# A graph network on one core: unscaled second 16-bit parts in the build, and a new order at the layer changes and at the end of attention

## The chip, the cores and the metric

One Trainium2 chip, one of its cores (core 0). The metric is the device time of one execution of the program in microseconds (us).

## What is computed

Four residual blocks on x (2048 nodes x 512) over 67584 edges that are sorted by target (65536 random ones and 2048 loops). Each starts with h = max(layernorm(x), 0):

```python
x = x + attention(h)            # 32 graphs of 64 nodes, 8 heads; biases edge_attr @ We + be
                                # are added to the scores at (graph, source, target) of each edge
x = x + gcn3(h)                 # three times A1 @ (h @ W) + b, relu between; A1 from degrees
x = x + relu(A2 @ (h @ W.T + b))
x = x + relu(A3 @ (h @ weight)) # A3: edge_weight summed by (row, column)
```

## The kernel before

The nodes are 16 tiles of 128 (NT). 32-bit values that go through cheap products are held as two 16-bit parts: a first part (value x scale, rounded) and a second part (what the rounding left).

**The build** (`build_*`, once in these runs) turns the edge list into dense matrices with products of one-hot matrices, while PE also computes attention's projections. 1024 units of two nodes lie in 8 groups of 128; a unit's edges lie on the 128 partitions, and 16 units are a batch: 64 batches, n = 0 to 63. Per batch and engine:
- DVE, `hots(n)`: five products or comparisons that make the one-hot matrices, for sources (L706), for counts and weights (L701, L714) and for biases (L704, L719). They are held twice (n % 2). Then `evacuate(n - 1)`: the bias sums (L731) and the weight sums (L747) leave PSUM, as second part / 2^11 + what ACT has copied.
- PE: `project` pieces (L979 for q and k up to batch 41, L972 for v after it; zero to two pieces a batch by a fixed table; each piece is four 32-bit products, issued as eight instructions), now and then the turning of h (`turn_h`, L954), then 16 products of 256 columns for the biases (L996), 16 of 96 columns for counts and weights (L1001), and the turning of sums (`turn_weights`, L945). At batches with n % 8 = 3 the next group's fields are turned too (L933), and with n % 8 = 0 there is one product for the in-degrees (L994). Before L996, PE waits until `hots(n)` is made and the bias sums of n - 1 have left PSUM; before L1001, until the weight sums of n - 1 have.
- ACT: it copies projected pieces, the first parts of the sums (`copy_sums`: L843 biases, L849 counts, L850 weights), turned sums (L837) and the normed h (`relu`, L854). At n % 8 = 3 it makes the first parts of the next group (`copy_part`, part 0, L825 and L826); at n % 8 = 5 DVE makes the rest in 32 bits in place (`residual`, L685 and L686), and ACT scales it by 2^11 (`copy_part`, part 1, again L825 and L826). DVE's next group waits for that.
- SP stores pieces and sums, and loads x and h.

The second part is scaled by 2^11 (LOW), so its sums can't be added to the first part's in PSUM: columns of both stand side by side in `hot_eb` and in the bank.

**Attention** (`attention_*`) runs in periods t over tiles: PE turns probabilities of t + 1 (L1311), projects tile t (`output`, L1341), mixes t + 1 (L1329) and scores t + 4 (L1300). In the last two periods ACT also prepares the first graph layer: in t = 14 four `weight_hi` (L1657) and two `relu` (L1673), ahead of the copy of the mixed tile 15 (`copy_mixed`, L1247) for which `output(15)` waits; in t = 15 `copy_turned` and `split_hi` for tiles 0 and 1, then two more `relu`. PE turns tiles 0 and 1 (L1866) ahead of `output(15)`, and 2 and 3 behind it.

**Layers** 0 to 4 each have `products` (h @ W; 12 products a tile, L1923: first x first, first x second, second x first) and `sums` (aggregation, L1989, 16 tiles x 2 parts x 16 blocks). In layers 1 and 2, h is split by a power of two that comes from its largest value: DVE's `h_scale` (L2171 and on), one `peak_row` (L1872) and one `peak_all` (L1879) on PE. The last of the four column chunks is scaled while products 0 to 2 run: after product 0 stands `peak_row`, after product 1 `peak_all`. PE asks for tile t + 1 two products before the end of tile t (`await_parts`): its second part, and the result of tile t - 2 having left its bank. ACT and DVE split tile 3 in their turn t = 3, after the results of tile 0. In layer 3 two products with one row of ones (L1919) put the bias into PSUM, one for each 16-bit part. `between` places single PE instructions among the sums by their number.

Of the kernel before, what the change touches and what calls it, by code (L numbers as in the profile page):

```python
# [18 lines left out]
H = 8  # L19
# [480 lines left out]
LOW = float(2 ** 11)  # L500
# [24 lines left out]
def build_memory(nc, keep, m):  # L525
# [11 lines left out]
    m.bias_first = place("bias_first", [P, NT, H], F32, AT_REST + 23040)  # L537
# [8 lines left out]
    m.bias_new = m.stage[:, 0:2].rearrange("p z (two t h) -> p z two t h", two=2, h=H)[:, :, 0]  # L546
# [5 lines left out]
BUILD_SEMS = "got read turned copied rest keyed parts hots batch bias_done first_part first_bias slab biased chunk new dve store0 store1"  # L552
# [103 lines left out]
def build_dve(nc, io, keep, m, s, first_round):  # L656
# [64 lines left out]
    def evacuate(n):  # L721

        nonlocal k
        q = n // 4
        sums = m.bias_ps[:, 0:NT * HP].rearrange("p (t two h) -> p two t h", t=NT, two=2)
        out = keep.bias[:].rearrange("p (h t) m -> p t h m", h=H)[:, :, :, n]
        dve.wait_ge(s["first_bias"], n + 1)
        if n % NBATCH == 0:
            dve.tensor_tensor(keep.deg[:], m.deg_ps.rearrange("q (c b) -> q b c", c=CPT), keep.deg[:], ALU.add)
        if first_round:  # L730
            dve.scalar_tensor_tensor(out, sums[:, 1], 1.0 / LOW, m.bias_first[:], ALU.mult, ALU.add).then_inc(s["biased"], 1)  # L731
        else:
            new = m.bias_new[:, n % 2]
            dve.scalar_tensor_tensor(new, sums[:, 1], 1.0 / LOW, m.bias_first[:], ALU.mult, ALU.add).then_inc(s["dve"], 1)
            k += 1
            dve.wait_ge(s["dve"], k)
            dve.tensor_tensor(out, new, out, ALU.add).then_inc(s["biased"], 1)
        dve.wait_ge(s["first_part"], n + 1)
# [8 lines left out]
        dve.scalar_tensor_tensor(slab, m.cw_ps[:, :, 2 * CCOLS:CW], 1.0 / LOW, m.w_first[:], ALU.mult, ALU.add).then_inc(s["slab"], 1)  # L747
# [51 lines left out]
def build_act(nc, io, keep, m, s, first_round):  # L799
# [14 lines left out]
    def copy_part(t, part, piece=0):  # L814
# [4 lines left out]
        if part == 0:  # L819
            act.wait_ge(s["turned"], FGROUPS * (t + 1))  # L820
            if t >= 2:
                act.wait_ge(s["hots"], NBATCH * (t - 1))
        else:
            act.wait_ge(s["rest"], part_count(t, piece, first_round))
        act.activation(m.w_parts[:, z, units, part], weight, ACT.Copy, scale=LOW if part else keep.scale[:, 1:2])  # L825
        act.activation(m.eb_parts[:, z, units, part * H:(part + 1) * H], biases, ACT.Copy,  # L826
                       scale=LOW if part else keep.scale[:, 0:1]).then_inc(s["parts" if part else "copied"], 1)
# [56 lines left out]
    for piece in range(len(unit_parts(0, first_round))):  # L884
        copy_part(0, 0, piece)
    copy_part(0, 1)
# [3 lines left out]
    for n in range(LAST):  # L890
# [7 lines left out]
        if first_round and n == 0:  # L898
            copy_part(0, 1, 1)
        if first_round and n >= 4:  # L900
            copy_weights(n - 4)
        if t + 1 < GTILES:
            if i == 3:
                copy_fields(t + 1)
                copy_part(t + 1, 0)
            if i == 5:
                copy_part(t + 1, 1)
# [9 lines left out]
def build_pe(nc, io, keep, m, s, first_round):  # L917
# [64 lines left out]
    for n in range(LAST):  # L982
# [243 lines left out]
def attention_act(nc, io, keep, layers, m, s, tools):  # L1226
# [26 lines left out]
    for t in attention_periods():  # L1253
# [217 lines left out]
B_SCALE = 2.0 ** -5  # L1471

# [999 lines left out]
```

## Time and profile before

| | us |
|---|---|
| three runs | 1448.24, 1450.48, 1451.29; median 1450.48 |
| the profiled execution's own time | 1449.56 |
| its span, first to last instruction | 1448.3 |
| PE, DVE, ACT busy | 1389.9, 920.8, 557.1 |
| stages in the span, about | preparation 0 to 52, build 52 to 461, attention 461 to 573, layers 573 to 1448 |

A busy PE is not a PE at its peak: a product's row lasts until its result is out, and products overlap, so the chain of work that ended last, which counts from one start to the next, gives the price of a product in a row of them. A gap that a row of PE shows is short by that overhang, the 1.91 us of a group of 16 in the timeline against 1.75 in the chain.

### The profile page before, as it was taken

The page shows a single profiled execution, that of the slowest core. Times are in us where ns is not written, and L with a number is a line of the kernel's source. Part 1 is how long each engine was busy: PE and PEld are TensorE (multiplying, and loading weights), DVE is VectorE, ACT ScalarE, POOL GpSimd, SP SyncE. Part 2 cuts the span into 40 slices and gives each one's busy share as a digit, 9 for nine tenths or more (in the row PEclk, how much of TensorE's full clock was granted, in tenths as well). Part 3 has the DMA queues.
Part 4 walks back from the last instruction along what each step waited for, and adds up shares of the span by engine and source line. Part 5 has one row for each costly group of instructions (what it writes and reads, how often), then busy time and mean ns, then how long its engine had stood idle before and what let it go on. Part 6 is the DMA issues. An engine that isn't in the chain of part 4 may idle for free.

```text
span 1448.3 us, 22005 instructions
## 1 busy us (share of the span) xinstructions
PE 1389.9 (96%) x8879; PEld 839.2 (58%) x8879; DVE 920.8 (64%) x1463; ACT 557.1 (38%) x969; POOL 90.9 (6%) x85
## 2 busy tenths in 40 slices
PE   7699998999996999999999999999999999999998
PEld 7488887878886665544444444444444444444443
DVE  7999999899997887657664766543245223432322
ACT  2466566545543446721123112402244223422322
POOL 3211001001000211000000100002100000000000
PEclk9799999999998999999999999999999999999999
DMA  8533233354336661200000200003202123553201
GB/s 323 167 112 123 107 125 119 118 177 129 104 124 199 213 216 59 81 30 1 0 1 1 58 0 1 1 15 88 83 20 59 51 67 80 210 198 104 92 1 59
DMA packets 70073, 134.46 MB, mean 93 GB/s; under 512 B 11722, under 2 KB 24138, under 8 KB 68556
## 3 DMA queue, kind: packets, MB, share of 16 engines
q1 hardware_dynamic: 67828, 122.87, 25.6%
q0 software_dynamic: 1280, 5.77, 1.5%
q10 hardware_dynamic: 856, 4.33, 0.8%
q8 instruction: 73, 1.20, 0.3%
q14 instruction: 36, 0.29, 0.1%
HBM read 79.62 MB, written 53.32 MB: 92 GB/s over the span
## 4 chain that ended last, share of the span: by engine, by line
PE 76%; DVE 17%; issue 3%; ACT 2%; DMA 1%; POOL 0%; ACTq 0%; SPq 0%; DVEq 0%; POOLq 0%
PE banks L1989 28%; PE banks L1923 14%; PE banks L2053 11%; PE banks L979 4%; DVE x_sb L719 4%; PE banks L996 4%; PE banks L1341 4%; DVE x_sb L706 2%; PE banks L1001 1%; PE banks L1866 1%; DVE x_sb L714 1%; DVE w_slab L747 1%; DVE fields L686 1%; PE banks L1311 1%; PE banks L1300 1%
## 5 line engine op out<-in xcount | busy, mean ns | idle before, releaser
L1989 PE MATMUL banks<-g,count 128*128 128x512 f16 x1024 | 227.6, 379 | 0.5 <-DVE tiles L2252 0.5
L1989 PE MATMUL banks<-count,g 128*128 128x512 f16 x1024 | 223.7, 379 | 0.0
L1923 PE MATMUL banks<-w_parts,h_parts 128*128 128x512 f16 x960 | 215.2, 379 | 1.5 <-DVE h_parts L2140 0.9
L1989 PEld LDWEIGHTS banks<-count,g 128*128 128x128 f16 x1024 | 99.5, 98 | 118.1
L2053 PE MATMUL banks<-g,part 128*128 128x512 f16 x768 | 165.9, 379 | 0.0
L1989 PEld LDWEIGHTS banks<-g,count 128*128 128x128 f16 x1024 | 99.8, 98 | 113.5 <-DVE tiles L2252 1.0
L1923 PEld LDWEIGHTS banks<-w_parts,h_parts 128*128 128x128 f16 x960 | 91.2, 98 | 118.2 <-issue 12.9
L719 DVE TENSOR_TENSOR x_sb<-eb_parts,x_sb 128x4096 f16<-128x4096 f16 x64 | 146.1, 2283 | 0.0
L996 PE MATMUL banks<-x_sb 128*128 128x256 f16 x1024 | 125.1, 276 | 6.5 <-DVE bias L731 6.5
L2053 PEld LDWEIGHTS banks<-g,part 128*128 128x128 f16 x768 | 75.1, 98 | 90.6
L996 PEld LDWEIGHTS banks<-x_sb 128*128 128x128 f16 x1024 | 100.1, 99 | 28.2 <-DVE x_sb L719 6.1
L2333 DVE SCALAR_TENSOR_TENSOR part<-count,e_scale,part 128x1024 f16<-128x1024 f32 x29 | 37.2, 1284 | 105.9 <-ACT part L1819 105.9
L1793 ACT ACTIVATE h_gcn_t<-h_gcn_t,b_col,unscale 128x512 f32<-128x512 f32 x32 | 26.0, 813 | 170.1 <-DVE h_gcn_t L2244 170.1
L706 DVE TENSOR_TENSOR x_sb<-iota_src,keys 128x2048 f16<-128x2048 f16 x64 | 77.8, 1216 | 0.0
L1819 ACT ACTIVATE part<-count,e_scale 128x1024 f16<-128x1024 f32 x29 | 33.3, 1148 | 110.9 <-PE banks L2053 110.9
L2142 DVE TENSOR_TENSOR h_parts<-h_gcn_t,h_parts 128x512 f16<-128x512 f32 x48 | 39.4, 823 | 51.4 <-ACT h_parts L1704 51.4
L2203 DVE SCALAR_TENSOR_TENSOR g<-banks,g_scale,g 128x512 f16<-128x512 f32 x64 | 47.8, 747 | 26.0 <-ACT g L1727 26.0
L979 PE MATMUL banks<-h_t,wq_sb 128*128 128x256 f32 x256 | 59.7, 381 | 0.0
L979 PE MATMUL banks<-h_t,wk_sb 128*128 128x256 f32 x256 | 59.4, 380 | 0.2 <-ACT fields L811 0.2
L1341 PE MATMUL banks<-wo_sb,att_t 128*128 128x512 f32 x128 | 59.2, 606 | 0.3 <-ACT att_t L1247 0.2
L1727 ACT ACTIVATE g<-banks,g_scale 128x512 f16<-128x512 f32 x64 | 43.4, 678 | 38.8 <-PE banks L1923 31.6
L2256 DVE TENSOR_TENSOR tiles<-tiles,banks 128x512 f32<-128x512 f32 x16 | 11.0, 687 | 68.0 <-ACT banks L1797 68.0
(303 smaller groups left out, 1931.6 us busy)
## 6 DMA issues: line engine op xcount, KB each, us to landing
weight_dram<-w_new SPq DMA_DIRECT2D x62, 256.0 KB, 2.4
count<-weight_dram SPq DMA_DIRECT2D x29, 512.0 KB, 7.1
qk_dram<-stage SPq DMA_DIRECT2D x64, 128.0 KB, 1.9
tiles<-x_dram SPq DMA_DIRECT2D x32, 256.0 KB, 3.5
x_dram<-tiles SPq DMA_DIRECT2D x32, 256.0 KB, 2.8
count<-in_x SPq DMA_DIRECT2D x4, 1024.0 KB, 12.2
h<-in_x SPq DMA_DIRECT2D x16, 256.0 KB, 3.7
h_dram<-h_t SPq DMA_DIRECT2D x8, 512.0 KB, 3.0
```

The lines of the kernel that those rows point to most:

```text
L706: dve.tensor_tensor(m.hot_src[:, z].rearrange("p g (c two) -> p g c two", two=2), keep.iota_src[:].rearrange("p (c two) -> p c two", two=2 ...
L719: dve.tensor_tensor(m.hot_eb[:, z].rearrange("p g (t c) -> p g t c", t=NT), values, tiles, ALU.mult).then_inc(s["hots"], 1)
L979: mm = pe.matmul(m.work_ps[:, bank, 0:SCOLS], weights[:, k, c * P:(c + 1) * P], m.h_t[:, k, :], start=k == 0, stop=k == KT - 1)
L996: mm = pe.matmul(m.bias_ps[:, 0:NT * HP], m.hot_src[:, z, g], m.hot_eb[:, z, g], start=g == 0, stop=g == BATCH - 1)
L1341: mm = pe.matmul(m.wo_ps[:, t % 2], m.att_t[:, k, :], keep.wo[:, k, :], start=k == 0, stop=k == KT - 1)
L1727: act.activation(m.g[:, t, 0], prod_bank(m, layer, t), ACT.Copy, scale=scale).then_inc(s["ghi"], 1)
L1923: mm = pe.matmul(out, m.h_parts[:, slot, zh, k], m.w_parts[:, zw, k], start=n == 0 and layer != 3, stop=n == len(passes) - 1)
L1989: mm = pe.matmul(m.agg_ps[:, b], lhs, rhs, start=i == 0 and z == 0, stop=i == NT - 1 and z == 1)
L2053: mm = pe.matmul(m.banks[:, b], m.part[:, n % 3, z, b * P:(b + 1) * P], m.g[:, q, gz], start=q == 0 and (z, gz) == (0, 0), stop=q == NT - ...
L2142: dve.tensor_tensor(out, source, hi, ALU.subtract).then_inc(s["lo"], 1)
L2203: dve.scalar_tensor_tensor(lo, result, scale, hi, ALU.mult, ALU.subtract).then_inc(s["glo"], 1)
L2333: dve.scalar_tensor_tensor(m.part[:, n % 3, 1], raw_place(m, n), m.e_scale[:, 0:1], m.part[:, n % 3, 0], ALU.mult, ALU.subtract).then_inc( ...
```

## The change

In the build the second part keeps the first part's scale and is made by DVE straight into 16 bits; both parts' products add into the same 128 columns. In the first round ACT alone moves the bias sums out. The in-degree product writes beside the counts. The rest moves instructions, and layer 3's bias becomes one product of 33 rows, of which two are not zero.

```diff
-    m.deg_ps = keep.banks[0:2 * GTILES, 7, NT * HP:NT * HP + P]
+    m.deg_ps = m.cw_ps[0:2 * GTILES, 0:GROUPS, CW:P]
...
     def residual(t, piece=0):
-        weight, biases = m.fields[:, 2, units], m.fields[:, 3:FIELDS, units]
+        weight = m.fields[:, 2, units].unsqueeze(2).to_broadcast([P, units.stop - units.start, 2])
+        biases = m.fields[:, 3:FIELDS, units].rearrange("p h u -> p u h")
         dve.wait_ge(s["copied"], part_count(t, piece, first_round))
-        dve.scalar_tensor_tensor(weight, weight, keep.scale[:, 1:2], m.w_parts[:, z, units, 0, 0], ALU.mult, ALU.subtract)
-        dve.scalar_tensor_tensor(biases, biases, keep.scale[:, 0:1], m.eb_parts[:, z, units, 0:H].rearrange("p u h -> p h u"),
-                                 ALU.mult, ALU.subtract).then_inc(s["rest"], 1)
+        dve.scalar_tensor_tensor(m.w_parts[:, z, units, 1], weight, keep.scale[:, 1:2], m.w_parts[:, z, units, 0], ALU.mult, ALU.subtract)
+        dve.scalar_tensor_tensor(m.eb_parts[:, z, units, H:HP], biases, keep.scale[:, 0:1], m.eb_parts[:, z, units, 0:H],
+                                 ALU.mult, ALU.subtract).then_inc(s["parts"], 1)
...
     def evacuate(n):
-        dve.wait_ge(s["first_bias"], n + 1)
+        dve.wait_ge(s["first_part"], n + 1)
         if n % NBATCH == 0:
...
-        if first_round:
-            dve.scalar_tensor_tensor(out, sums[:, 1], 1.0 / LOW, m.bias_first[:], ALU.mult, ALU.add).then_inc(s["biased"], 1)
...
-        dve.scalar_tensor_tensor(slab, m.cw_ps[:, :, 2 * CCOLS:CW], 1.0 / LOW, m.w_first[:], ALU.mult, ALU.add).then_inc(s["slab"], 1)
+        dve.tensor_tensor(slab, m.cw_ps[:, :, 2 * CCOLS:CW], m.w_first[:], ALU.add).then_inc(s["slab"], 1)
...
     def copy_sums(n):
-        act.wait_ge(s["bias_done"], n + 1)
-        if n:
-            act.wait_ge(s["biased"], n)
-        act.copy(m.bias_first[:], m.bias_ps[:, 0:NT * HP].rearrange("p (t two h) -> p two t h", t=NT, two=2)[:, 0]).then_inc(s["first_bias"], 1)
+        if first_round:
+            act.wait_ge(s["bias_done"], n + 1)
+            act.copy(keep.bias[:].rearrange("p (h t) m -> p t h m", h=H)[:, :, :, n],
+                     m.bias_ps[:, 0:NT * H].rearrange("p (t h) -> p t h", h=H)).then_inc(s["biased"], 1)
...
-            if i == 5:
-                copy_part(t + 1, 1)
...
         if n:
             pe.wait_ge(s["biased"], n)
-        if i == 0:
-            pe.matmul(m.deg_ps, keep.half_of[:, GTILES - 1 - t:3 * GTILES - 1 - t], keep.match[:], start=True, stop=True)
         for g in range(BATCH):
-            mm = pe.matmul(m.bias_ps[:, 0:NT * HP], m.hot_src[:, z, g], m.hot_eb[:, z, g], start=g == 0, stop=g == BATCH - 1)
+            parts = m.hot_eb[:, z, g].rearrange("p (t two h) -> p two t h", two=2, h=H)
+            for part in range(2):
+                mm = pe.matmul(m.bias_ps[:, 0:NT * H], m.hot_src[:, z, g], parts[:, part], start=g == part == 0,
+                               stop=g == BATCH - 1 and part == 1)
         mm.then_inc(s["bias_done"], 1)
         if n:
             pe.wait_ge(s["slab"], n)
+        if i == 0:
+            pe.matmul(m.deg_ps, keep.half_of[:, GTILES - 1 - t:3 * GTILES - 1 - t], keep.match[:], start=True, stop=True)
...
         if t == NT - 2:
-            for k in range(KT):
-                tools.weight_hi(0, k)
             tools.relu(0, 0)
             tools.relu(0, 1)
+            tools.weight_hi(0, 0)
         if is_tile(t + 1):
             copy_mixed(t + 1)
+        if t == NT - 2:
+            for k in range(1, KT):
+                tools.weight_hi(0, k)
...
         if t == NT - 1:
+            tools.relu(0, 2)
+            tools.relu(0, 3)
             for u in range(2):
                 tools.copy_turned(0, u)
                 tools.split_hi(0, u)
-            tools.relu(0, 2)
-            tools.relu(0, 3)
...
-                if t >= 2 and layer not in (0, 4):
+                if t >= 2 and layer not in (0, 4) and (layer == 3 or t != 3):
                     split_hi(layer, t)
+                if t == 2 and layer in (1, 2):
+                    split_hi(layer, 3)
...
         if layer == 3:
-            for z in range(2):
-                pe.matmul(out, m.b_ones[:], m.b_parts[:, z], start=z == 0, stop=False)
+            pe.matmul(out, m.b_ones[:], m.b_parts[:], start=True, stop=False)
         for n, (zh, k, zw) in enumerate(passes):
...
+            if layer in (1, 2) and (t, n) == (1, 1):
+                peak_row()
+            if layer in (1, 2) and (t, n) == (2, 1):
+                peak_all()
...
-            if layer in (1, 2) and t == 1:
-                peak_row()
-            if layer in (1, 2) and t == 2:
-                peak_all()
...
-            if layer == 2 and n == 24:
+            if layer == 2 and n == 26:
                 peak_row()
-            if layer == 2 and n == 29:
+            if layer == 2 and n == 31:
                 peak_all()
...
         elif layer < 2:
-            if n == (22 if c == 1 else 8):
+            if n == (22 if c == 1 else 9):
                 peak_row()
-            if n == (28 if c == 1 else 14):
+            if n == (28 if c == 1 else 15):
                 peak_all()
...
-            elif t < NT and t >= (3 if layer < 3 else 2):
+            elif t < NT and t >= 2 and (layer == 3 or t > 3):
                 split_lo(layer, t)
+            elif t == 2:
+                split_lo(layer, 3)
```

Left out are the later rounds (not run here: every batch's rows stand 64 times) and the tiles of 33 rows for `b4_row`, `b_parts` and `b_ones`.

## Rows read from the trace of the kernel before

**Rows 1.** The page: the chain that ended last, shares of the span by engine.

```profile
PE 76%; DVE 17%; issue 3%; ACT 2%; DMA 1%; POOL 0%; ACTq 0%; SPq 0%; DVEq 0%; POOLq 0%
```

**Rows 2.** The chain in the build (start, us, what): PE's price of each group.

```profile
120.49 0.87 PE banks L954 x8
...
171.30 1.75 PE banks L996 x16
173.05 0.68 PE banks L1001 x16
173.73 0.51 PE banks L945 x4
```

**Rows 3.** The chain in the build where DVE carries it: from one batch to the next.

```profile
378.54 2.20 DVE x_sb L719
380.74 0.29 DVE bias L731
...
383.95 2.20 DVE x_sb L719
```

**Rows 4.** Groups by form, 40 to 620 us: the operations that the build loses or changes.

```profile
L996 PEld LDWEIGHTS banks<-x_sb 128*128 128x128 f16 x1024 | 100.1, 99 | 28.2 <-DVE x_sb L719 6.1 <-issue 4.7
L747 DVE SCALAR_TENSOR_TENSOR w_slab<-banks,w_first 128x512 f32<-128x512 f32 x64 | 43.5, 680 | 12.1 <-ACT w_first L850 11.9
L826 ACT ACTIVATE eb_parts<-fields,scale 128x1024 f16<-128x1024 f32 x7 | 14.5, 2078 | 0.0
L686 DVE SCALAR_TENSOR_TENSOR fields<-fields,scale,eb_parts 128x1024 f32<-128x1024 f32 x7 | 14.5, 2077 | 0.0
L1406 DVE TENSOR_TENSOR x_sb<-x_sb,banks 128x512 f32<-128x512 f32 x16 | 10.9, 680 | 0.6 <-PE banks L1341 0.6
```

**Rows 5.** Timeline of the build: PE's stops (start, us, group, idle before and its releaser).

```profile
198.02 1.91 PE L996 MATMUL banks<-x_sb 128*128 128x256 f16 x16 [0.49 <-DVE bias L731]
...
250.53 0.63 PE L954 MATMUL banks<-ident,h 128*128 128x128 f32 x4 [3.23 <-ACT h L854]
...
252.41 3.00 PE L996 MATMUL banks<-x_sb 128*128 128x256 f16 x16
...
447.34 0.68 PE L945 MATMUL banks<-ident,w_slab 128*128 128x128 f32 x4
...
450.32 1.91 PE L996 MATMUL banks<-x_sb 128*128 128x256 f16 x16 [2.30 <-DVE bias L731]
```

**Rows 6.** Waits, 57 to 456 us (who, for whom, us in total, times, longest).

```profile
PE banks L996 <- DVE bias L731: 6.5, 9, 2.3
```

**Rows 7.** The chain at attention's end.

```profile
555.82 3.70 PE banks L1341 x8
...
564.44 1.11 ACT w_parts L1657 x2
...
566.90 1.41 ACT h_gcn L1673 x2
...
569.36 5.02 PE banks L1341 x8
...
575.26 2.59 PE banks L1923 x12
```

**Rows 8.** The chain at the start of layer 1.

```profile
747.42 0.75 DVE g L2203
748.17 0.67 DVE h_parts L2140
```

**Rows 9.** Waits, 456 to 1448 us, PE only: its stops at peaks.

```profile
PE banks L1872 <- DVE peak L2171: 1.2, 4, 0.3
...
PE banks L1872 <- DVE peak L2290: 0.8, 1, 0.8
```

**Rows 10.** The chain in layer 3's products: the bias and a tile.

```profile
1068.46 0.53 PE banks L1919 x2
1069.00 2.70 PE banks L1923 x12
```

More of the change, by code:

```diff
@@ L536, in build_memory @@
     m.w_first = place("w_first", [P, BATCH, CCOLS], F32, AT_REST + 20992)
-    m.bias_first = place("bias_first", [P, NT, H], F32, AT_REST + 23040)
     m.w_new = place("w_new", [P, 2, 512], F32, AT_REST + 23552)
@@ L545, in build_memory @@
     m.w_old = m.h_t[:].rearrange("p k n -> p (k n)").rearrange("p (z c) -> p z c", z=2)
-    m.bias_new = m.stage[:, 0:2].rearrange("p z (two t h) -> p z two t h", two=2, h=H)[:, :, 0]
     m.work_ps, m.bias_ps = keep.banks[:, 0:WORK], keep.banks[:, 7]
-    m.deg_ps = keep.banks[0:2 * GTILES, 7, NT * HP:NT * HP + P]
     m.cw_ps = keep.banks[:, WORK:7].rearrange("p b (g c) -> p (b g) c", c=P)
-BUILD_SEMS = "got read turned copied rest keyed parts hots batch bias_done first_part first_bias slab biased chunk new dve store0 store1"
+    m.deg_ps = m.cw_ps[0:2 * GTILES, 0:GROUPS, CW:P]
+BUILD_SEMS = "got read turned copied keyed parts hots batch bias_done first_part slab biased chunk new dve store0 store1"
 FIRST_SEMS = "new_late"
@@ L721, in evacuate @@
     def evacuate(n):
-        nonlocal k
         q = n // 4
-        sums = m.bias_ps[:, 0:NT * HP].rearrange("p (t two h) -> p two t h", t=NT, two=2)
-        out = keep.bias[:].rearrange("p (h t) m -> p t h m", h=H)[:, :, :, n]
-        dve.wait_ge(s["first_bias"], n + 1)
-        if n % NBATCH == 0:
-            dve.tensor_tensor(keep.deg[:], m.deg_ps.rearrange("q (c b) -> q b c", c=CPT), keep.deg[:], ALU.add)
-        if first_round:
-            dve.scalar_tensor_tensor(out, sums[:, 1], 1.0 / LOW, m.bias_first[:], ALU.mult, ALU.add).then_inc(s["biased"], 1)
[L732 to L738, printed above, removed]
+        if not first_round:
+            out = keep.bias[:].rearrange("p (h t) m -> p t h m", h=H)[:, :, :, n]
+            dve.wait_ge(s["bias_done"], n + 1)
+            dve.tensor_tensor(out, m.bias_ps[:, 0:NT * H].rearrange("p (t h) -> p t h", h=H), out, ALU.add).then_inc(s["biased"], 1)
+        dve.wait_ge(s["first_part"], n + 1)
+        if n % NBATCH == 0:
+            part = CPT // GROUPS
+            dve.tensor_tensor(keep.deg[:].rearrange("q b (g c) -> q b g c", c=part), m.deg_ps.rearrange("q g (c b) -> q b g c", c=part),
+                              keep.deg[:].rearrange("q b (g c) -> q b g c", c=part), ALU.add)
         if not first_round:
@@ L812, in copy_fields, with copy_part @@
                      m.work_ps[:, bank, 0:n * P].rearrange("p (f g) -> p f g", f=n)).then_inc(s["turned"], 1)
-    def copy_part(t, part, piece=0):
+    def copy_part(t, piece=0):
         z, units = t % 2, unit_parts(t, first_round)[piece]
@@ L818, in copy_part @@
         biases = m.fields[:, 3:FIELDS, units].rearrange("p h u -> p u h")
[L819 to L827, printed above, removed]
+        act.wait_ge(s["turned"], FGROUPS * (t + 1))
+        if t >= 2:
+            act.wait_ge(s["hots"], NBATCH * (t - 1))
+        act.activation(m.w_parts[:, z, units, 0], weight, ACT.Copy, scale=keep.scale[:, 1:2])
+        act.activation(m.eb_parts[:, z, units, 0:H], biases, ACT.Copy, scale=keep.scale[:, 0:1]).then_inc(s["copied"], 1)
     def copy_weights(c):
@@ L884, in build_act @@
     for piece in range(len(unit_parts(0, first_round))):
-        copy_part(0, 0, piece)
-    copy_part(0, 1)
+        copy_part(0, piece)
     if first_round:
@@ L897, in build_act @@
         copy_sums(n)
-        if first_round and n == 0:
-            copy_part(0, 1, 1)
         if first_round and n >= 4:
@@ L904, in build_act @@
                 copy_fields(t + 1)
-                copy_part(t + 1, 0)
-            if i == 5:
-                copy_part(t + 1, 1)
+                copy_part(t + 1)
         if n + 1 < LAST:
@@ L1471 @@
 B_SCALE = 2.0 ** -5
+BROWS = P // 4 + 1
 def slots(layer):
@@ L1501, in layers_memory @@
     m.b3_row = place("b3_row", [P, D], F32, AT_REST + 20480)
-    m.b4_row = place("b4_row", [1, D], F32, AT_REST + 22528)
-    m.b_parts = place("b_parts", [1, 2, D], F16, AT_REST + 24576)
-    m.b_ones = place("b_ones", [1, P], F16, AT_REST + 26624)
+    m.b4_row = place("b4_row", [BROWS, D], F32, AT_REST + 22528)
+    m.b_parts = place("b_parts", [BROWS, D], F16, AT_REST + 24576)
+    m.b_ones = place("b_ones", [BROWS, P], F16, AT_REST + 26624)
     m.stats = place("stats2", [P, 8 * PER], F32, AT_REST + 26880)
@@ L2120, in weight_spread @@
             settle(dve.tensor_scalar(m.unscale[:, 3:4], m.w_scale[:, 3, 1:2], H_SCALE, None, ALU.mult))
-            settle(dve.tensor_scalar(m.b4_row[:], m.b4_row[:], m.w_scale[0:1, 3, 0:1], B_SCALE, ALU.mult, ALU.mult))
-            settle(dve.tensor_copy(m.b_parts[:, 0], m.b4_row[:]))
-            dve.tensor_tensor(m.b_parts[:, 1], m.b4_row[:], m.b_parts[:, 0], ALU.subtract).then_inc(s["b_scaled"], 1)
+            settle(dve.tensor_scalar(m.b4_row[:], m.b4_row[:], m.w_scale[0:BROWS, 3, 0:1], B_SCALE, ALU.mult, ALU.mult))
+            settle(dve.tensor_copy(m.b_parts[:], m.b4_row[:]))
+            last = slice(BROWS - 1, BROWS)
+            dve.tensor_tensor(m.b_parts[last], m.b4_row[last], m.b_parts[last], ALU.subtract).then_inc(s["b_scaled"], 1)
     def weight_lo(layer, k):
@@ L2334, in split_raw @@
                                  ALU.mult, ALU.subtract).then_inc(s["part"], 1)
-    dve.memset(m.b_ones[:], 2.0 ** 15)
+    settle(dve.memset(m.b_ones[:], 0.0))
+    for row in (0, BROWS - 1):
+        dve.memset(m.b_ones[row:row + 1], 2.0 ** 15)
     for layer in range(4):
```

5 lines of the change are left out of this document (2 added, 3 removed).

## The prediction, made before the changed kernel was run

> **What bounds the kernel now.** I read the page's chain first: PE carries 76% of the span, DVE 17%, ACT 2% [rows 1]. DVE's share lies nearly all in the build, so there I read the chain in short windows. In stretches PE's groups follow each other without a break, the 16 bias products at 1.75 us, the 16 count and weight products at 0.68 [rows 2]; in other stretches DVE's operations do, at 383.95 - 378.54 = 5.41 us a batch, of which the bias evacuation L731 is 0.29 [rows 3]. Both engines are close to full: the reader should see two co-bounds that wait for each other only now and then. So what matters is PE's idle time, not DVE's work. In the timeline of the build PE stops nine times for L731, 6.5 us in all [rows 6]: five times before the last k piece at 318 us (2.4 us together, 198.02 is one), three times in the v part (1.7), and 2.3 before the last batch [rows 5]. It stops 3.2 us at 250.53 for ACT's relu of h, and the 16 products behind that stop take 3.00 instead of 1.91 us [rows 5], at a granted clock of half speed. Behind the build PE is continuous but for short stops at the layer changes and the end of attention.
>
> **The build: PE's products.** 16 products of 256 columns become 32 of 128. The same streams give the price of a product: 1.75/16 = 109 ns for 256 columns and 0.68/16 = 42.5 ns for 96 [rows 2], each with its own weight load. The line between them is 0.42 ns a column and 2.5 ns for each product. At 128 columns that makes 56 ns, and 32 x 56 = 1.79 us a batch, 0.04 more than now. From below, the price can't be under 32 x 53 = 1.71 (the columns still stream). From above: a weight load lasts 99 ns [rows 4]; if loads couldn't hide one behind the other, 32 x 99 = 3.2 us. I take 1.79, since L1001's pairs run at 42.5 ns with the same load. The Trainium skill ("TensorE: Matmul & The Clock Gate", section "Back-to-back issue gap") says otherwise: load and product pairs of 128 columns sustain about 81 ns each. By that the batch would take 2.6 us, 0.84 more, and the 64 batches some 54 us; the 42.5 ns of L1001 speak against it.
>
> The moving operand is now read in runs of 8 values of 16 bits with gaps of 8. No row shows that. The nearest is a weight load with a stride: L945's four turns take 0.51 (128 ns each), L954's unstrided eight 0.87 (109 ns) [rows 2], 17% more, one value at a time. I take nothing, since here 8 neighbours are used, and keep 17% (+0.3 us a batch) for the upper end. The Trainium skill ("SBUF — State Buffer", in "Door 1: The DMA port swizzle") has lines of 16 bytes whose repeated use is free; 8 values fill one, so by it the price is nothing too, and L945's 17% agrees with its penalty for a new line each time.
>
> **The build: DVE and ACT.** L731 goes from DVE, 0.29 us a batch [rows 3]. The weight evacuation changes from a scaled add to an add of the same operands: L747 has 680 ns, L1406 (an add from PSUM) 680 [rows 4], nothing. The residual now reads fields with a stride and writes 16 bits. ACT does just this in 2078 ns, DVE's present form takes 2077 [rows 4]: nothing, with 7 x 1 us either way as bounds, and seven times some 0.1 more for the doubled weight. ACT loses its second copy, about 2.4 us per group; its bias copy now writes with a stride, but starts when L996 ends, while PE still has 0.68 us of L1001 ahead of ACT's next copy, so even twice the time hides. The in-degree product and its add only change places. Nothing on SP's or POOL's queue moves.
>
> What PE gets back, in order:
> - The five waits before 318 us: PE now needs `hots(n)` and ACT's early copy, not DVE's late evacuation. 2.4 us, plus 0.16 each that the modelled end hides (1.91 against 1.75) = **3.2**.
> - The stop at 250.53: ACT's second copy (2.4 us) and its wait for DVE's residual stood ahead of relu. Without them relu ends before PE's pieces do. 3.2 + 0.3 for the second turn + 2 x 0.16 + (3.00 - 1.91) for the clock = **5.0**.
> - The v part: PE is ready for the last batch at 447.34 + 0.52 = 447.9, but starts at 450.3 [rows 5]. DVE gets there 20 x 0.29 = 5.8 earlier, at about 444.2; PE gets ready 1.7 + 3 x 0.16 earlier by its own waits and 22 x 0.04 = 0.9 later by its products, at 446.6, perhaps 446.0 with stops too short to be listed. PE is last; 450.3 - 446.3 = **4.0**.
> - PE's longer batches before 318: 41 x 0.04 = **-1.6**.
> Build: -10.6 us.
>
> **End of attention.** The chain runs through ACT: four weight splits (564.44 to 566.90), two relus (1.41), the mixed copy (up to 569.36), then `output(15)`, 5.02 us long where a tile before took 3.70, and product 0 at 575.26 [rows 7]. After the change: relus from 564.44 to 565.85, one split to 566.5, the copy to 567.55; output starts 1.75 us earlier and ends at 571.2 at full clock. But ACT then has three splits (to 569.4), two relus (570.8) and two pairs of copy and split of 1.1 us; PE's turn of tile 3 needs the second copy (572.5) and takes 0.45. So product 0 starts at 573.0: ACT is late next, not PE. **-2.3 us**; 1.7 if the clock drops again, 3 at best.
>
> **Layers 1 and 2, start.** DVE's result of tile 0 (747.42, 0.75) and then the split of tile 3 (748.17, 0.67) end PE's wait [rows 8]. In the new order the split runs while ACT makes its half of the result; the result is last, at 748.17. ACT's split of tile 3 waits for product 1, and what queues behind it (ACT's result 0) needs a later scale anyway. PE resumes 0.67 earlier, twice: **-1.3**. The two stops at peaks there (0.3 each, two of the four in [rows 9] and those of `peak_all`) are ahead of this wait, so moving them gives nothing more.
>
> **Peaks among sums.** Two stops for the third chunk, 0.3 each, and the one of 0.8 in layer 2 [rows 9] vanish, since one or two products (0.22 each) run first: **-1.4**.
>
> **Layer 3's bias.** Two products take 0.53 of a tile's 3.23 [rows 10]; one takes half, 0.22 to 0.27, whatever its rows. 16 x 0.24 = 3.8. In four tiles, those where ACT has a relu between, the second part is ready only 0.1 before it is used, so about 0.1 each is lost: **-3.4**. The table of zeros and ones costs DVE two memsets where it waits.
>
> **Sum.** 10.6 + 2.3 + 1.3 + 1.4 + 3.4 = 19.0 us. The profiled execution took 1449.56, which makes 1430.6; it stands 0.9 below the median of the three runs. Forecast 1430.5, own range 1425 to 1436.
>
> **Rivals.**
> - *PE keeps the build.* The stops at L731 become stops for the hots or for L747's evacuation, which DVE still does behind the residual, and the strided residual costs up to 1 us more a group, on DVE's path. Then the build gives 0 to 3 and the rest 8.4: 1438 to 1441. For it: PE's rows follow each other nearly everywhere. Against it: L747 is needed only 1.75 us after L731 was.
> - *The narrow products cost more* (slower). Place: the 32 bias products of each batch, on PE, the fuller engine. It decides from 56 + 19.0/63/32 = 65 ns a product; at 17% for the stride (66 ns) the gain is just gone, 1450; with unhidden loads it is (3.2 - 1.79) x 63 = 89 us more, 1520. By the skill's 81 ns it would be about 1480. Against it stands L1001.
> - *The change does only half at attention's end and in the layers*: the same waits, one instruction later. 1434, inside my range.
>
> **How the numbers follow.** The forecast's own case, with the half of the third rival, 0.76; PE keeps the build 0.12; narrow products dearer 0.12, of which 0.10 slower and 0.02 within 0.2% (2.9 us, about what a measurement here can tell from no change). The range 1424 to 1441 takes in the first two and leaves out the last. Faster 0.88, same 0.02, slower 0.10.
>
> **What would show it.** Right: 32 bias products in 1.8 us in the chain; no wait of PE on L731's place; no stop at relu of 3 us; PE, not DVE, nearly alone in the build's chain; the first layer's product 2.3 us sooner after the build's end; 2.96 a tile in layer 3. Wrong: a group of bias products of 2 us or more, a residual of 3 us, or new waits of PE on DVE's weight evacuation.

## The result and the profile after

The changed kernel took 1435.3 us, the median of four runs (1432.9 to 1436.2), beside 1450.8 for the kernel before in the same comparison: ratio 0.9894, 95% interval 0.9877 to 0.9911, faster by 15.5 us. Five later runs beside other kernels gave a median of 1433.4 (1432.9 to 1437.0). The forecast was 1430.5, its range 1424 to 1441. The time lies in both ranges that the prediction states (1424 to 1441, and 1425 to 1436), the sign is right, and the gain is 3.5 us smaller than the sum of 19.0 said.

The profiled execution took 1435.73, with a span of 1434.5. Page of the changed kernel: the chain by engine, then three groups of the build (answer to [rows 1] and [rows 4]).

```profile
PE 88%; DVE 6%; ACT 3%; issue 2%; DMA 1%; POOL 0%; ACTq 0%; SPq 0%; POOLq 0%
...
L979 PE MATMUL banks<-x_sb 128*128 128x128 f16 x2048 | 126.5, 220 | 4.3 <-DVE x_sb L717 4.3
...
L739 DVE TENSOR_TENSOR w_slab<-banks,w_first 128x512 f32<-128x512 f32 x64 | 43.7, 682 | 24.3 <-ACT w_first L838 24.3
L830 ACT COPY bias<-banks 128x128 f32<-128x128 f32 x64 | 24.6, 385 | 87.4 <-PE banks L979 87.2
```

PE went from 76% of the chain to 88%, DVE from 17% to 6%. The add of L739 costs what the scaled one did (682 against 680 ns). ACT's copy of the bias sums got slower (385 ns, 265 before) and hides: ACT waits 87 us for PE ahead of it over the build.

The chain in the build of the changed kernel (start, us, what), as in [rows 2]:

```profile
92.02 1.79 PE banks L979 x32
93.80 0.68 PE banks L987 x16
94.48 0.52 PE banks L928 x4
```

The 32 products last 1.79 us. The timeline where PE stopped for relu before, and at the last batch [rows 5]:

```profile
246.96 1.04 PE L937 MATMUL banks<-ident,h 128*128 128x128 f32 x8
...
247.83 1.95 PE L979 MATMUL banks<-x_sb 128*128 128x128 f16 x32
...
442.77 1.96 PE L979 MATMUL banks<-x_sb 128*128 128x128 f16 x32 [1.77 <-DVE x_sb L717]
```

The eight turns of h run without a stop, at the full granted clock (1.00 in this stretch). Waits of the changed kernel in the build, 57 to 456 us, PE's and DVE's (who, for whom, us in total, times, longest):

```profile
PE banks L979 <- DVE x_sb L717: 4.3, 4, 1.8
```

```profile
DVE w_slab L739 <- ACT w_first L838: 24.3, 21, 3.3
```

No wait of PE for the bias copy is left where [rows 6] had nine; PE's longest waits are now for the one-hots (`x_sb`). The second row says that DVE, ahead of its weight evacuation, waits for ACT's copy of the weight sums; the kernel before has 11.9 us there, in 14 waits. The prediction had not asked for it.

To see the build by itself I take distances between the starts of groups of bias products, since they don't depend on when an execution begins. Here and below batches count from 0; batch 41 is the first behind a piece of v, 63 the last.

| us | before | changed | its second profile |
|---|---|---|---|
| batch 2 to 41 | 252.42 | 245.69 | 245.09 |
| batch 41 to 63 (v part) | 126.03 | 124.64 | 124.64 |
| batch 63 to attention's first product | 10.74 | 10.40 | 10.19 |

One part of the first row changes from profile to profile: a stop of PE just before the first piece of v, whose releaser the trace doesn't show. It is 2.35 us before, 2.00 and 1.40 in the changed kernel's two profiles, and 1.4 to 3.0 in the others below.

The end of attention in the changed kernel, timeline (before: [rows 7]):

```profile
560.60 3.70 PE L1329 MATMUL banks<-wo_sb,att_t 128*128 128x512 f32 x8 [0.22 <-ACT att_t L1233]
...
566.00 2.75 PE L1913 MATMUL banks<-w_parts,h_parts 128*128 128x512 f16 x12
...
570.30 0.11 DVE L2328 MEMSET b_ones<- 33x64 uint32 x1
570.49 0.39 DVE L2330 MEMSET b_ones<- 1x128 f16 x2
570.89 0.69 DVE L2133 TENSOR_TENSOR h_parts<-h_gcn_t,h_parts 128x512 f16<-128x512 f32 x1
...
572.40 2.75 PE L1913 MATMUL banks<-w_parts,h_parts 128*128 128x512 f16 x12 [0.18 <-DVE g L2194]
```

`output(15)` takes 3.70 instead of 5.02, so the clock doesn't fall here any more, and product 0 follows 5.40 behind its start (5.73 in the timeline of before). The third product, though, follows 11.80 behind it, as before (11.79): what is gained at product 0 is lost again by then, mostly at DVE's writes of `b_ones` (run 10). The chains at layer 1's start and in layer 3, for [rows 8] and [rows 10]:

```profile
738.32 0.76 DVE g L2194
```

```profile
1050.56 0.32 PE banks L1909
1050.88 2.69 PE banks L1913 x12
```

At layer 1's start DVE's result of tile 0 now ends PE's wait by itself, and one bias product of 33 rows takes 0.32.

### The profile page after: what moved, and what is told of

It reads as the page before. It is cut to its first block, busy times and chain, and to the rows that moved or that the text cites. A ratio compares the mean times of both kernels' runs of the same rounds, so it can differ in the third digit from the quotient of the medians.

```text
span 1434.5 us, 23871 instructions
## 1 busy us (share of the span) xinstructions
PE 1385.5 (97%) x9887; PEld 854.0 (60%) x9887; DVE 906.6 (63%) x1401; ACT 548.5 (38%) x951; POOL 94.6 (7%) x85
## 4 chain that ended last, share of the span: by engine, by line
PE 88%; DVE 6%; ACT 3%; issue 2%; DMA 1%; POOL 0%; ACTq 0%; SPq 0%; POOLq 0%
PE banks L1979 31%; PE banks L1913 13%; PE banks L2043 11%; PE banks L979 7%; PE banks L962 7%; PE banks L1329 3%; PE banks L955 3%; PE banks L987 3%; PE banks L928 2%; PE banks L1857 1%; PE banks L1299 1%; DVE x_sb L717 1%; PE banks L1288 1%; PE banks L1317 1%; PE banks L290 1%
## 5 line engine op out<-in xcount | busy, mean ns | idle before, releaser
L979 PE MATMUL banks<-x_sb 128*128 128x128 f16 x2048 | 126.5, 220 | 4.3 <-DVE x_sb L717 4.3
L979 PEld LDWEIGHTS banks<-x_sb 128*128 128x128 f16 x2048 | 120.9, 99 | 13.3 <-DVE x_sb L717 5.6
L2326 DVE SCALAR_TENSOR_TENSOR part<-count,e_scale,part 128x1024 f16<-128x1024 f32 x29 | 37.2, 1284 | 105.9 <-ACT part L1810 105.9
L739 DVE TENSOR_TENSOR w_slab<-banks,w_first 128x512 f32<-128x512 f32 x64 | 43.7, 682 | 24.3 <-ACT w_first L838 24.3
L830 ACT COPY bias<-banks 128x128 f32<-128x128 f32 x64 | 24.6, 385 | 87.4 <-PE banks L979 87.2
```

Of the source, the lines that this page charges most:

```text
L739: dve.tensor_tensor(slab, m.cw_ps[:, :, 2 * CCOLS:CW], m.w_first[:], ALU.add).then_inc(s["slab"], 1)
L979: mm = pe.matmul(m.bias_ps[:, 0:NT * H], m.hot_src[:, z, g], parts[:, part], start=g == part == 0, stop=g == BATCH - 1 and part == 1)
```

## The experiments

Each kernel is the changed one with one edit, unless it says that it starts from the kernel before.

**1 and 2. The halves alone.** From the kernel before, the build's part only:

```diff
+            for part in range(2):
+                mm = pe.matmul(m.bias_ps[:, 0:NT * H], m.hot_src[:, z, g], parts[:, part], start=g == part == 0,
+                               stop=g == BATCH - 1 and part == 1)
...
```

(`residual`, `evacuate`, `copy_part`, `copy_sums` and `deg_ps` are the changed ones; nothing behind the build is.)

> The build as changed, attention and layers as before. My theory after reading the trace of the changed kernel: the build gives about 7.5 us to the start of attention, attention then gives 0.8 back because its half-speed stretch of the clock lies later in it; so 6 to 8 us less than before, the last group of bias products at about 443 us, and the end of attention 7.0 us earlier, with output(15) again at 5.0 or at 3.7 us. Rival (the parts lean on each other: the earlier build changes what the end of attention costs): the sum of this gain and of the gain of the other half alone misses 15.5 us by more than 2 us.

And from the kernel before, the order at attention's end, in the layers and layer 3's bias, without the build:

```diff
-            for k in range(KT):
-                tools.weight_hi(0, k)
...
+            pe.matmul(out, m.b_ones[:], m.b_parts[:], start=True, stop=False)
...
```

(Every later hunk of the diff is in it, the build's are not.)

> The build as before, attention's end, layers and layer 3's bias as changed. Theory: 1.7 us at the end of attention plus 1.6 for the clock that no longer drops there, 1.1 in the first products of layers 1 and 2, 1.4 at the peaks, 2.6 in layer 3: 6.8 to 8.4 us less than before. Rival (what looks like the layers' gain is only the build's shift): under 5 us.

Measured: 1441.4 (ratio 0.9937, 0.9922 to 0.9951) and 1444.4 (0.9961, 0.9947 to 0.9976), beside 1450.6. That is 9.2 and 6.3 us, together the whole of 15.5: the parts add, as far as intervals of some 2 us either way can tell. The first is more than the 6 to 8 expected, the second less than the 6.8 to 8.4. (The profile of the first half is of its slowest run, 1446.0.) The second half keeps every stop in the build, such as this one in its timeline:

```profile
251.03 0.63 PE L954 MATMUL banks<-ident,h 128*128 128x128 f32 x4 [3.21 <-ACT h L854]
```

The first half has none of them, and at attention's end it has the drop of the clock:

```profile
565.01 5.40 PE L1327 MATMUL banks<-wo_sb,att_t 128*128 128x512 f32 x8 [0.34 <-ACT att_t L1233]
```

The second half's profile has none there, and neither has any other profile of a kernel with the new order (twelve in all); the two without it both have it. So the full clock at attention's end goes with the reordering, not with the shorter build.

**3. ACT's second copy put back.** ACT reads the second parts and writes them onto themselves behind DVE's residual; the values stay.

```diff
+    def copy_back(t, piece=0):
...
+        act.wait_ge(s["rest"], part_count(t, piece, first_round))
+        act.copy(m.w_parts[:, z, units, 1], m.w_parts[:, z, units, 1])
+        act.copy(m.eb_parts[:, z, units, H:HP], m.eb_parts[:, z, units, H:HP]).then_inc(s["parts"], 1)
```

> The changed kernel with ACT's second copy put back: after DVE's residual ACT copies both second parts onto themselves, and DVE's next one-hots wait for it. Theory (this copy and its wait for DVE stood ahead of relu): PE stops again for about 3 us at a turning of h near 250 us, the clock drops behind it, and the kernel is 4 to 5.5 us slower than the changed one, so 10 to 11.5 below before; elsewhere in the build no new stops of PE. Rival (that stop came from DVE's heavier batches, and went with them): no stop above 1 us there, and 15 us below before as the changed kernel.

Measured: 1437.9 (1436.7 to 1439.0; ratio 0.9916, 0.9900 to 0.9931), 2.6 above the changed kernel, less than the 4 to 5.5 expected. Batch 2 to 63 is 374.24 us where the changed kernel has 370.33, 3.9 more. Its timeline:

```profile
246.51 0.41 ACT L820 COPY w_parts<-w_parts 128x256 f16<-128x256 f16 x1 [2.41 <-DVE eb_parts L684]
246.82 1.04 ACT L821 COPY eb_parts<-eb_parts 128x1024 f16<-128x1024 f16 x1
247.77 1.52 ACT L848 ACTIVATE h<-h,shift,rstd 128x512 f32<-128x512 f32 x2
248.72 2.09 PE L948 MATMUL banks<-ident,h 128*128 128x128 f32 x8 [2.35 <-ACT h L848]
...
250.61 2.68 PE L990 MATMUL banks<-x_sb 128*128 128x128 f16 x32
```

The stop is back at this one place, with the slow products behind it (2.68 instead of 1.95). It is 0.9 shorter than before because a copy within 16 bits takes 1.04 where the old one took 1.97. The larger part of what ACT costs is its 2.41 us of waiting for DVE's residual while relu stands behind.

**4. DVE moves the bias sums out again**, ACT doesn't.

```diff
     def evacuate(n):
+        else:
+            out = keep.bias[:].rearrange("p (h t) m -> p t h m", h=H)[:, :, :, n]
+            dve.wait_ge(s["bias_done"], n + 1)
+            dve.tensor_copy(out, m.bias_ps[:, 0:NT * H].rearrange("p (t h) -> p t h", h=H)).then_inc(s["biased"], 1)
...
     def copy_sums(n):
-        if first_round:
-            act.wait_ge(s["bias_done"], n + 1)
-            act.copy(keep.bias[:].rearrange("p (h t) m -> p t h m", h=H)[:, :, :, n],
-                     m.bias_ps[:, 0:NT * H].rearrange("p (t h) -> p t h", h=H)).then_inc(s["biased"], 1)
```

> The changed kernel with the bias sums moved by DVE again (a plain copy, at its old place behind the next one-hots and the residual) and not by ACT. Theory (PE's waits came from DVE's late evacuation, and it cost DVE 0.2 to 0.3 us a batch): PE stops for the bias evacuation return, 4 to 6 us in all, the last group of bias products comes 4 to 6 us later than in the changed kernel, and the whole stands 9.5 to 11.5 us below before. Rival (PE's groups bind the build, DVE's part does not matter): within 1.5 us of the changed kernel, 14 to 15.5 below before.

Measured: 1443.3 (1438.2 to 1443.8; ratio 0.9952, 0.9936 to 0.9967), 8 above the changed kernel. PE's waits in its build:

```profile
PE banks L979 <- DVE bias L729: 6.1, 8, 2.3
```

The waits of [rows 6] (6.5 us, nine of them) are back. Batch 41 to 63 is 126.64, batch 2 to 63 is 375.38, 5.0 longer than in the changed kernel, of which 0.8 is a longer stop before the first piece of v (2.81). That is as much as the theory said. The median is 3 us worse than that. The profile is of the run at 1438.2, whose mean granted clock is 0.988; the three others, at 1443.1 to 1443.8, have 0.984. So some of those 3 us may be time at half clock, but no trace of such a run was kept, and they stay open.

**5. Bias products that read columns lying together.**

```diff
-            parts = m.hot_eb[:, z, g].rearrange("p (t two h) -> p two t h", two=2, h=H)
+            parts = m.hot_eb[:, z, g].rearrange("p (two c) -> p two c", two=2)
```

> The changed kernel, but each bias product reads 128 columns that lie together in hot_eb instead of sixteen runs of eight 128 elements apart (so it sums columns of the wrong grouping; the output is not the reference's; the number of products and their columns are the same). Theory, that the gathered reading costs TensorE nothing: a batch's 32 bias products take 1.79 us as in the changed kernel, the last group of the build ends at the same distance from its first within 0.3 us, and the time is 1435 within 2. Rival, that the stride costs and other work hid it: the 32 products take under 1.5 us and the time falls by 1 to 5 us where DVE is not the bound.

Measured: one run at 1438.1, batch 2 to 63 in 370.06 (370.33 in the changed kernel), and in the chain:

```profile
93.98 1.79 PE banks L979 x32
```

The runs of eight values cost TensorE nothing that the trace shows. The time is 3 us above the theory's 1435 and 2.3 above the changed kernel's profiled run, and these 2.3 lie elsewhere: batch 2 begins 2.0 us later in this execution, and attention's first product comes 0.7 later behind batch 63.

**6. Weights ahead of counts on ACT.** I had now read the row of 24.3 us, and took DVE's wait for `w_first` as what eats the v part's gain.

```diff
+        if first_round and n >= 44:
+            act.wait_ge(s["first_part"], n + 1)
...
+            act.activation(to_count, m.w_first[:].rearrange("p (c b) (h s) -> p s c b h", c=GROUPS, h=2), ACT.Copy,
+                           scale=2.0 ** -14).then_inc(s["tallied"], 1)
```

> The changed kernel, but from batch 44 on ACT writes a batch's weights before the count values and takes the latter from the weights in SBUF, so the weights come one count copy (0.58 us) earlier than now and ACT's total work stays within a tenth (the counts of these batches come out as other numbers than the reference's, and go nowhere that sets a time). Theory, that in the v part DVE waits for ACT's w_first behind the count copy (24.3 us over the build where it was 11.9 before): these waits shrink from batch 44 on by over half, the last bias group of the build ends 1.5 to 3 us sooner, about 1432 to 1434. Rival, that DVE's own row of instructions at 5.21 us a batch sets the v part and the waits only stand where it had time: under 0.5 us, 1435. A second rival, that ACT's whole row is full there: the wait moves to the bias copy and PE stops for its banks, 1435 to 1438.

Measured: 1436.3 (1432.8 to 1437.5), batch 41 to 63 in 124.29, 0.35 less. The theory fell: ACT's copy of the weights starts with the end of PE's counts now, one copy sooner, but DVE's waits for it are 24.5 us, no less than in the changed kernel. PE's stops before batches 55 and 63 shrink by 0.5 each (0.62 to 0.15, 1.77 to 1.28), and a stop at the turning of the fields grows by 0.6 (0.26 to 0.88).

**7. Work put in place of the wait.**

```diff
-            hots(n + 1)
+            hots(n + 1, left)
...
+        if between is not None:
+            evacuate(between)
```

> The changed kernel, but in the build DVE sums batch n's four gathered eighths between the two comparisons of batch n+2's hots, where it now waits for ACT's weights, instead of ahead of both. Nothing is left out. Theory, that DVE's waits for w_first in the v part stand behind ACT's latency, and that work put in their place hides it: the hots of the v part come at 5.21 us or less, 1 to 3 us come off the build's end, 1432 to 1434.5. Rival, that the summing itself is late for what waits behind it (ACT's h copy and the product of h with the weights): the gathering's banks come free later and PE stops 1 to 2 us for them in some batches, 1436 to 1439.

Measured: 1434.9 (1433.6 to 1435.2; ratio 0.9887, 0.9871 to 0.9904). Batch 41 to 63 took 123.98, 0.66 less; the stop before the first piece of v was as much longer (2.65 for 2.00). No difference to the changed kernel can be told.

**8. Less DVE work in the v part.** After runs 6 and 7 the next theory was that PE itself is full there and that DVE waits for ACT only because ACT waits for PE.

```diff
+        light = first_round and n > 43
+        if not light:
+            dve.tensor_tensor(cw[:, :, 0:CCOLS].rearrange("p g (c two) -> p g c two", two=2),
+                              keep.iota_cnt[:].rearrange("p (c two) -> p c two", two=2).unsqueeze(1).to_broadcast([P, BATCH, NT, 2]),
+                              key(1, CCOLS), ALU.is_equal).then_inc(s["dve"], 1)
```

> The changed kernel, but from batch 44 on DVE leaves out the comparison of the counts' columns (L699, 0.41 us a batch; the counts of these batches then come from an earlier batch's columns, and the output is not the reference's). That takes 20 x 0.41 = 8.2 us from DVE in the v part and nothing from PE. Theory, that PE's row is what sets the v part and DVE's waits for w_first are waits for PE in the end: the groups of bias products up to batch 62 start where they do now within 0.7 us, DVE's waits for w_first grow by 5 us or more, and only the last stop before batch 63 (1.77 us) goes, 1433.0 to 1434.5. Rival, that DVE with ACT's copy in its path sets the v part: the last group of bias products comes 4 to 8 us sooner, 1427 to 1431.

Measured: one run at 1432.0; batch 41 to 63 in 123.29, 1.35 less for 8.2 us less work. The waits of DVE in its build:

```profile
DVE w_slab L741 <- ACT w_first L840: 28.8, 22, 3.4
DVE deg L731 <- ACT w_first L840: 3.1, 3, 1.4
```

The second row was 2.3 in the changed kernel, so DVE waits 5.3 us more: most of what it no longer has to do. From batch 41 to 62 the groups of bias products lie 0.7 us closer, not the 4 to 8 of the rival, so this settles it. What came back are the stops of PE at batch 55 (0.62) and a part of the last (1.77 to 1.10); the theory had the last one gone. The time itself, one run, is lower than the theory's by what lies outside the v part: compared with the profile of the changed kernel, attention took 1.2 less (half clock for 13.65 us in this execution, 17.07 there), and the storing of the results behind PE's last product 1.1 less (3.9 for 5.0).

**9. The pieces of v spread to the last batch.** If PE is full to batch 62 and idle before 63, work belongs there.

```diff
-V_BATCHES = LAST - 1 - V_START
+V_BATCHES = LAST - V_START
```

> The changed kernel, but the 32 pieces of v (8 products, 1.89 us each) are spread over the 23 batches 41 to 63 instead of the 22 batches 41 to 62, so the last piece stands before batch 63's bias products, where PE now stops 1.77 us for DVE's x_sb. Nothing is left out. Theory, that PE is full from batch 44 to 62 and idle only there: the last group of bias products starts 1 to 1.8 us sooner after the first one than now (382.7 us), 1433.5 to 1434.3. Rival, that the last piece's copy, its store or the reading back of v is late for attention: the distance from the last group of the build to attention's first product (10.4 us) grows by as much, 1435 or more.

Measured: 1437.2 (1435.4 to 1439.8; ratio 0.9909, 0.9897 to 0.9922), slower than the changed kernel by 2 to 4. Batch 41 to 63 took 123.50, so the stop went as the theory said. In the profile, which is of the slowest run (1439.8), the stretch before it grew by more: the stop before the first piece of v is 2.97, the granted clock is at half from 316.8 to 320.2 us behind it, and batch 2 to 41 takes 248.36, 2.7 more than in the changed kernel. Run 11, with the same table of pieces, has no such fall of the clock and takes 245.95 there, so it isn't the edit's price in every execution. What both have lies behind the build: from batch 63 to attention's first product it is 12.71 us, 2.3 more, and that product's successor waits 2.5 us where it waited 1.0. SP's queue, the chain and PE's waits there:

```profile
445.19 0.43 SPq L1059 DMA_DIRECT2D wo_sb<-in_L_gnn_Wo  x1
445.67 0.56 SPq L1077 DMA_DIRECT2D qk_second<-qk_dram  x1
448.58 0.32 SPq L1010 DMA_DIRECT2D weight_dram<-w_new  x1
```

```profile
448.58 8.11 DMA weight_dram<-w_new
```

```profile
PE banks L1288 <- issue: 5.9, 1, 5.9
PE banks L1288 <- DVE prob L1363: 2.5, 1, 2.5
```

Behind the store of the last piece, two loads of 1 MB stand in SP's queue. In the changed kernel they are issued at 438.82 and 442.74, and the weights' store at 447.13. Here all three lie within 3.4 us, the store takes 8.11 to land (a median of 2.4 over the 62 such stores of the changed kernel), and DVE, which reuses its buffer, waits; its first step on the scores (`prob`) comes late by that, and PE waits 2.5 us for it. What the first product's wait of 5.9 stands for (3.6 in the changed kernel) the trace doesn't show. That the loads slow the store is read from their order; no run moved them alone. DVE's wait for the store is 8.1 and 7.4 us in the two profiles with the spread pieces and 2.7 to 6.2 in those of the other edits of the changed kernel, so the order is not all of it.

**10. The memsets behind the first chunk.**

```diff
+                if layer == 0:
+                    settle(dve.memset(m.b_ones[:], 0.0))
+                    for row in (0, BROWS - 1):
+                        dve.memset(m.b_ones[row:row + 1], 2.0 ** 15)
...
-    settle(dve.memset(m.b_ones[:], 0.0))
-    for row in (0, BROWS - 1):
-        dve.memset(m.b_ones[row:row + 1], 2.0 ** 15)
```

> The changed kernel, but the three memsets of b_ones stand in layer 0's sums behind the first chunk instead of between attention's end and its third product. Theory, that they lie on the chain there (0.07, 0.17 and 0.17 us in the chain of waits at 570.35 to 570.88): 0.3 to 0.45 us off, nearly below what a measurement tells, but the third product of the profile stands 0.3 to 0.45 us nearer to the second than now. Rival, as the prediction had it, that they cost nothing: the distance between output(15) and the third product stays within 0.1 us.

Measured: 1435.0 (1433.3 to 1437.2), which tells nothing. In the profile the turns of h behind the third product start 14.04 us after `output(15)`, in the two profiles of the changed kernel 14.38 and 14.39: 0.34 us less, and PE's stop for `g` is gone. The memsets did lie on the path.

**11 and 12. Runs 7, 9 and 10 together, and the changed kernel again.**

> The three placements together: the sums of the gathered eighths inside hots, the b_ones memsets behind layer 0's first chunk, the pieces of v over 23 batches. If they add (0 to 0.5, 0.4 and 1 to 1.8 us): 1432.5 to 1434. If DVE's earlier row and the spread pieces cover the same stop: 1434 to 1435.

> The changed kernel itself once more, beside the others of this call on the same chip, to see what 1 or 2 us between them mean: 1435 within 1.5.

Measured: 1438.2 (1436.6 to 1441.5; ratio 0.9922, 0.9910 to 0.9934) and 1433.4 (1432.9 to 1437.0; ratio 0.9896, 0.9883 to 0.9910). The combination is slower than the changed kernel by 3 to 5: run 9's loss at attention's start is in it (batch 63 to attention's first product 12.19 us). No version tried beats the changed kernel by what can be measured.

## Why the prediction was right, and where it was off

**PE's products: right.** 1.79 us for 32, as the line between 256 and 96 columns gave; the weight loads hide, and run 5 shows the reading in short runs to be free. That is 56 ns for a pair of load and product at 128 columns. The page "TensorE: Matmul & The Clock Gate" (section "Back-to-back issue gap") of the Trainium skill would have had 81 and a slower kernel; no row here bears that out. The Trainium skill's rule on 16-byte lines ("SBUF — State Buffer", in "Door 1: The DMA port swizzle") agrees with run 5.

**The waits before the v part: right.** 3.2 + 5.0 - 1.6 = 6.6 expected; batch 2 to 41 lost 6.7, of which 0.35 is a shorter stop before the first piece of v. Runs 3 and 4 show both mechanisms. Between them a part of the 5.0 turned out to be ACT's wait for the residual rather than its copying.

**The v part: the step that failed.** Expected 4.0, measured 126.03 - 124.64 = 1.4. "DVE gets there 20 x 0.29 = 5.8 earlier, at about 444.2" treats DVE's row as if it ran by itself. Counted from the start of batch 41, that put DVE's last one-hots at 119.9 us and PE's readiness for them at 122.3 or sooner; in the changed kernel PE is ready at 122.7, but DVE only at 124.6. DVE's row doesn't run by itself: its weight evacuation of a batch waits for ACT's copy, and that for PE's products of the same batch, and the hots of the batch after next can't start before it. The chain of the changed kernel (start, us, what), from PE's counts of batch 60 to PE's start of batch 63:

```profile
430.39 0.69 PE banks L987 x16
...
431.58 0.60 ACT w_first L838
...
432.21 0.69 DVE w_slab L739
...
435.30 2.20 DVE x_sb L717
...
440.51 2.21 DVE x_sb L717
...
442.77 1.96 PE banks L979 x32
```

A DVE with less to do therefore waits more (11.9 to 24.3 us in the build, 29 in run 8) and can't get further ahead of PE. At the end PE has two batches with one piece of v each, 4.7 us apart, while DVE needs 5.2; so PE still ends in a stop, 1.77 for 2.30. "PE gets ready at 446.6" was off too: one new stop of 0.62 at batch 55 stands where two of 0.5 were. Busy time by window in the kernel before (stretch, its length, then busy us and instructions of each engine, granted clock, DMA):

```profile
350.00:400.00 50.00, 49.03 (x425) 43.26 (x424) 49.96 (x69) 27.28 (x54) 0.00 (x0) 1.00 0.33 110
```

```profile
400.00:445.00 45.00, 43.94 (x382) 38.41 (x381) 45.00 (x60) 21.88 (x47) 0.00 (x0) 1.00 0.34 112
```

PE, the first of the five, was busy 93.0 of these 95 us, DVE, the third, all of them. DVE was indeed the fuller one; but with its load lightened PE's 2.0 us are all that could come back here, wherever DVE got to. The window ends before the last stop. All of PE's stops for DVE in the v part are 4.0 us before (0.7, 0.5, 0.6 and 2.3) and 2.4 in the changed kernel (0.6 and 1.8). So the forecast of 4.0 took all of PE's idle time as won; over half of it stayed, and most of that in the last stop, which hangs on the last few batches and not on DVE's load over the whole part.

**The end of attention: mechanism right, size a little off.** Output comes 1.7 sooner (expected 1.75), product 0 2.0 (expected 2.3), and ACT's late splits, not PE, set it. "The table of zeros and ones costs DVE two memsets where it waits" is wrong by 0.34: it doesn't wait there, DVE's residual and statistics and then the memsets are the chain to the third product.

**Layers 1 and 2: right in kind.** Expected 1.3 at the starts, measured 2 x 0.57; the peaks among the sums gave 1.6 for 1.4 (0.43, 0.43 and 0.74).

**Layer 3's bias: a size.** One product is 0.32, not the half of 0.53, so a tile saves 0.21, and the four tiles where PE waits for the second part save nothing (3.68 us each, as before); together 2.6, not 3.4. The chain's 0.53 for two products did not say what one alone costs.

**The sum** of the profiled executions: of 19.0 expected, 13.8 came. Missing are 2.6 (v part), 0.8 (layer 3), 0.6 (end of attention), 0.4 (build and layer starts), 0.6 (this build starts late by that much), 0.8 of attention's first stretch, which differs from run to run, and 0.2 behind PE's last product; 0.7 came unasked at the stops before v and before attention, and 0.2 more than forecast at the peaks.

**The rivals.** Narrow products dearer: no. PE keeps the build: in its letter no, since 8.1 us came from batch 2 to 63; but it is right in the v part, for a reason it didn't name. Half only at attention's end and in the layers: no. That part gave 6.3 alone (3.5 to 7.7 by the interval), and 6.8 of its 8.4 in the profiles. The rival's time, 1434 (1434.7 by the prediction's own 8.4 / 2), is nearer to the measured one than the forecast's, but by luck: most of what is missing lies in the v part.

## What to carry to other kernels

When two engines are both nearly full and each waits for the other's last batch, work taken from one comes back at most as far as the other has idle time: read the busy share of both in that stretch first, and cap the gain with it. The cap is not yet the forecast (here 4.0 us of idle time gave 1.4): for each stop, ask what the lightened engine itself waits for. A wait that sits between two engines (DVE for ACT) may be the image of a third one being full; following the row one releaser further is cheaper than an experiment. And filling an idle stretch with compute moves what stands behind that compute, here two loads in front of the store that the next stage waits for.

## What the runs showed of the hardware

The weight load and product of 128 columns in 16 bits sustain 56 ns a pair, in groups of 32 (1.79 us) and over all 2048 of them but for PE's stops, also when the moving operand is read in runs of eight values. The half-speed stretch of the granted clock around attention's start lasted 17.07 us in one profile of the same kernel (1435.73 us) and 13.65 in another (1432.92), and attention's first 95 us came out 95.60 and 94.45: attention began 1.6 us later in the slower one, and the two together are the whole distance between the runs. Over all twelve profiles with the new order, the distance from attention's first product to `output(15)` is 105.9 to 106.3 us where this stretch lasts 13.65, 106.9 to 107.9 where it lasts 17.07, and 108.0 and 109.0 in the two where it lasts 20.48. Such differences between executions are as large as some of the terms that the prediction had worked out to a tenth.
